# A gated cross-attention layer: the first loads in another order, two chunks of each half of x normalised by GpSimd, tables with gaps

## The reference

```
xn   = layernorm(x)
q    = rope(einsum(xn @ Wq.T, w_kc_q))           # 16 heads, 192 wide
kv   = rope(ctx)                                 # 64 wide
attn = softmax((q @ W_qr) @ (kv @ W_kr).T)
x    = x + tanh(g_xattn) * ((attn @ kv) @ w_kc_kv.T) @ Wo.T
p    = softmax(layernorm(x) @ router.T + bias)   # 64 experts, top 8
x    = x + tanh(g_ffn) * (layernorm(x) * sum(top8) + top8 @ expert_bias)
```

## Time and profile before

| | us |
|---|---|
| median of 3 timed runs | 270.83 (270.72 to 271.25) |
| the profiled execution | 271.7 |
| its span, first to last instruction | 269.9 |
| TensorE busy | 257.0 (95%), 1825 matmuls |
| VectorE busy | 187.4 (69%) |
| ScalarE busy | 152.9 (57%) |
| GpSimd busy | 139.5 (52%) |
| DMA moved | 12.50 MB |

### The profile page before, as it was taken

The page is one execution under the profiler, slowest core; times in us unless marked ns, Lnnn a source line. Parts: engine busy times, 40 slices in busy tenths (PEclk is TensorE's granted clock), DMA queues, the critical chain, the costliest instruction groups (busy, mean ns, idle before and its releaser), DMA issues.

```text
span 269.9 us, 5396 instructions
## 1 busy us (share of the span) xinstructions
PE 257.0 (95%) x1825; PEld 195.6 (72%) x1825; DVE 187.4 (69%) x434; ACT 152.9 (57%) x440; POOL 139.5 (52%) x223
## 2 busy tenths in 40 slices
PE   7899799999999999999999999999999999999963
PEld 7674678578867888587848888577848756888751
DVE  3689978485864877287829956488728956777675
ACT  2531574686545646375555575636646558878541
POOL 3197038623690468326652755337451883447353
PEclk9999799999999999999999999999999999999999
DMA  7995030415000000051000300000000000000103
GB/s 234 223 295 159 1 97 2 138 45 142 2 0 0 2 0 4 1 183 42 0 2 0 100 1 2 0 0 2 0 4 0 2 2 0 2 0 2 39 2 117
DMA packets 15434, 12.50 MB, mean 46 GB/s; under 512 B 4592, under 2 KB 14704, under 8 KB 15408
## 3 DMA queue, kind: packets, MB, share of 16 engines
q1 hardware_dynamic: 14304, 11.37, 15.2%
q10 hardware_dynamic: 1104, 0.79, 1.0%
HBM read 11.11 MB, written 1.05 MB: 45 GB/s over the span
## 4 chain that ended last, share of the span: by engine, by line
PE 74%; DVE 7%; POOL 6%; DMA 4%; issue 3%; ACT 3%; ACTq 1%; POOLq 0%; DVEq 0%
PE ring L1033 22%; PE context L1209 10%; PE probs_t L1191 9%; PE scores L1180 6%; PE scores L1181 5%; PE ring L1073 4%; PE ring L1059 4%; DMA rope_k_sb<-in_rope_k 4%; PE ring L999 3%; DVE q_stack L772 3%; PE ring L1094 2%; PE ring L1090 2%; PE ring L1092 2%; PE ring L1012 2%; PE ring L1022 2%
## 5 line engine op out<-in xcount | busy, mean ns | idle before, releaser
L596 POOL TENSOR_SCALAR probs<-probs,inv_sum 128x256 f32<-128x256 f32 x128 | 59.6, 480 | 82.7 <-DVE inv_sum L943 82.7
L540 POOL TENSOR_TENSOR roped<-roped,cross 128x512 f32<-128x512 f32 x47 | 59.9, 1296 | 22.9 <-DVE cross L786 22.7
L700 ACT ACTIVATE probs<-scores,neg_max 128x256 f32<-128x256 f32 x128 | 59.8, 476 | 14.9 <-DVE neg_max L937 14.6
L710 ACT COPY probs_t_sb<-probs_t 128x512 f32<-128x512 f32 x64 | 37.8, 590 | 39.8 <-PE probs_t L1191 39.2
L937 DVE TENSOR_REDUCE neg_max<-scores 128x2 f32<-128x512 f32 x64 | 43.3, 677 | 8.8 <-PE scores L1181 8.7
L1033 PE MATMUL ring<-xn_hi,a_hi 128*128 128x512 f32 x96 | 40.2, 418 | 0.0
L1191 PE MATMUL probs_t<-ident,probs 128*128 128x128 f32 x256 | 38.8, 274 | 0.2
L1180 PE MATMUL scores<-keys_hi,q_stack 128*128 128x256 f32 x128 | 38.1, 319 | 0.7 <-ACT probs L700 0.3
L772 DVE TENSOR_TENSOR q_stack<-ring,q_stack 64x512 fp32r<-64x512 f32 x32 | 22.0, 689 | 23.5 <-ACT q_stack L691 22.9
L785 DVE TENSOR_TENSOR roped<-ring,rope_q_sb 128x512 f32<-128x512 f32 x48 | 32.8, 684 | 7.1 <-PE ring L1033 6.6
L1033 PE MATMUL ring<-xn_hi,a_lo 128*128 128x512 f32 x96 | 37.7, 393 | 0.0
(11 more groups left out here) (105 smaller groups left out, 438.0 us busy)
## 6 DMA issues: line engine op xcount, KB each, us to landing
...
```

The source lines that it names most:

```text
L540: last = nc.gpsimd.tensor_tensor(roped[:, j, k, :], roped[:, j, k, :], cross[:, done % 2, j, :], ALU.add)
L596: last = nc.gpsimd.tensor_scalar(e, e, inv_sum[:, i % 4, half:half + 1], 1.0, ALU.mult, ALU.mult)
L700: last = nc.scalar.activation(probs[:, i % E_BUFS, half, :], scores[:, i % 2, half, :], ACT.Exp, bias=neg_max[:, i % 4, half:half + 1], ac ...
L710: nc.scalar.copy(probs_t_sb[:, i % T_BUFS], probs_t[:]).then_inc(probs_t_ready, 1)
```

## The change

SP now issues pair 1's key weights behind the query weights, then the context, the key tables, and only then the three query tables; ScalarE issues x (chunks 2, 3) and pair 0's key weights. The rows of rope_q_sb and w_qr_sb get a gap of 8 elements, so that a query table arrives in rows of 2 KB and not of 4 KB, and the rank weights in rows of 1.5 KB and not of 3 KB; the tables' layout in SBUF is indexed anew. In each half of x VectorE normalises chunks 0 and 1 (of four) and GpSimd adds eps, takes the power and normalises chunks 2 and 3, with a semaphore of its own, xn_by_pool. The order of pieces is new in the opening (among others, both key pieces behind the rank merge), in the slots and at the end. No matmul is added or taken away. Of the slots' lists the first two steps and the last are shown.

```diff
--- before.py
+++ after.py
@@ -34,6 +34,7 @@
 E_BUFS, T_BUFS = 4, 8
 BLOCK_OF = (0, 2, 1)
 SHARED_SUM = PC - 1
+PAD = 8
 LOWEST = float(np.finfo(np.float32).min)
 WARM_UP = 24
 LEAD = 2
@@ -59,9 +60,9 @@
 
 def pieces_before():
 
-    return [("n", 0), ("a", 0, 0), ("x", 0, 0), ("a", 0, 2), ("x", 0, 1), ("c",), ("a", 0, 3), ("a", 0, 1),
-            ("table", 0), ("half", 2), ("q", 0, 0, 0), ("q", 0, 0, 1), ("q", 0, 1, 0), ("table", 1), ("q", 0, 1, 1),
-            ("k", 1), ("table", 2), ("q", 0, 2, 0), ("q", 0, 2, 1), ("m", 0, 0), ("k", 0), ("n", 1), ("r", 0),
+    return [("n", 0), ("a", 0, 0), ("a", 0, 1), ("a", 0, 2), ("x", 0, 0), ("c",), ("a", 0, 3), ("x", 0, 1),
+            ("half", 2), ("table", 0), ("q", 0, 0, 0), ("table", 1), ("q", 0, 0, 1), ("table", 2), ("q", 0, 1, 0),
+            ("q", 0, 1, 1), ("q", 0, 2, 0), ("q", 0, 2, 1), ("m", 0, 0), ("k", 0), ("k", 1), ("n", 1), ("r", 0),
             ("p", 0), ("x", 1, 0), ("x", 1, 1), ("a", 1, 1)]
 
 
@@ -74,66 +75,66 @@
     (
         ([("a", 1, 0)], []),
         ([("q", 1, 0, 1)], [("q", 1, 1, 0)]),
-        ([("q", 1, 1, 1)], [("q", 1, 2, 0)]),
+        ([], [("q", 1, 1, 1), ("q", 1, 2, 0)]),
         ([("q", 1, 2, 1)], [("a", 1, 2), ("a", 1, 3)]),
         ([], [("r", 1), ("p", 1)]),
-        ([("o", 1, 0)], [("m", 1, 0)]),
-        ([], [("out", 0, 0, 2)]),
-        ([], [("q", 2, 0, 0)]),
+        ([("o", 1, 0)], []),
+        ([("m", 1, 0)], []),
+        ([("out", 0, 0, 2)], []),
     ),
     (
+        ([("q", 2, 0, 0)], []),
         ([], []),
-        ([], []),
-        ([("q", 2, 0, 1)], [("q", 2, 1, 0)]),
+        ([("q", 2, 0, 1), ("q", 2, 1, 0)], []),
         ([("q", 2, 1, 1)], [("q", 2, 2, 0)]),
-        ([("q", 2, 2, 1)], []),
+        ([], [("q", 2, 2, 1)]),
         ([("r", 2), ("p", 2)], [("out", 0, 2, 2)]),
-        ([("out", 1, 4, 2)], []),
-        ([("q", 3, 0, 0)], [("q", 3, 0, 1)]),
+        ([("out", 1, 4, 2)], [("q", 3, 0, 0)]),
+        ([("q", 3, 0, 1)], [("centre",), ("a", 2, 2)]),
     ),
...
     (
-        ([("turn", 0, 2)], []),
-        ([("root", 0, 2)], [("logit", 0, 2)]),
+        ([("root", 0, 2), ("turn", 0, 2)], []),
+        ([], [("logit", 0, 2)]),
         ([("out", 6, 2, 2)], []),
-        ([], [("take", 0, 2)]),
-        ([("turn", 2, 2)], [("pick", 0, 2), ("part", 0, 2), ("root", 2, 2)]),
-        ([], []),
-        ([("logit", 2, 2), ("out", 7, 4, 2)], []),
-        ([("turn", 4, 2), ("root", 4, 2)], [("take", 2, 2), ("mix", 0, 2), ("logit", 4, 2), ("take", 4, 2)]),
+        ([], [("turn", 2, 2), ("take", 0, 2)]),
+        ([("root", 2, 2)], [("pick", 0, 2)]),
+        ([("logit", 2, 2), ("part", 0, 2)], []),
+        ([("out", 7, 4, 2)], []),
+        ([("turn", 4, 2)], [("root", 4, 2), ("take", 2, 2), ("mix", 0, 2), ("logit", 4, 2), ("take", 4, 2)]),
     ),
 )
 
@@ -161,10 +162,10 @@
 
 def pieces_after():
 
-    return [("part", 2, 2), ("pick", 2, 2), ("pre", 7, 6, 2), ("out", 7, 6, 1), ("root", 6, 1), ("out", 7, 7, 1),
-            ("root", 7, 1), ("turn", 6, 1), ("part", 4, 2), ("logit", 6, 1), ("mix", 2, 2), ("take", 6, 1),
-            ("pick", 4, 2), ("part", 6, 1), ("turn", 7, 1), ("logit", 7, 1), ("take", 7, 1), ("pick", 6, 1),
-            ("mix", 4, 2), ("part", 7, 1), ("mix", 6, 1), ("pick", 7, 1), ("mix", 7, 1)]
+    return [("pick", 2, 2), ("part", 2, 2), ("pre", 7, 6, 2), ("out", 7, 6, 1), ("root", 6, 1), ("out", 7, 7, 1),
+            ("part", 4, 2), ("pick", 4, 2), ("root", 7, 1), ("turn", 6, 1), ("logit", 6, 1), ("take", 6, 1),
+            ("mix", 2, 2), ("turn", 7, 1), ("part", 6, 1), ("logit", 7, 1), ("pick", 6, 1), ("take", 7, 1),
+            ("mix", 4, 2), ("mix", 6, 1), ("pick", 7, 1), ("part", 7, 1), ("mix", 7, 1)]
 
 
 def ring_plan():
@@ -224,13 +225,13 @@
         x_sb = sb("x_sb", [P, CHUNKS, D])
         ctx_sb = sb("ctx_sb", [P, CHUNKS, DC])
         gates = sb("gates", [P, 2])
-        rope_q_sb = sb("rope_q_sb", [P, PC, 4, S])
+        rope_q_sb = sb("rope_q_sb", [P, PC, 2, 2 * S + PAD])
         rope_k_sb = sb("rope_k_sb", [P, 1, 2, 2, DC])
         wq_sb = sb("wq_sb", [P, GH, D])
         w_kc_q_sb = sb("w_kc_q_sb", [P, GH, CQ])
         w_kc_kv_sb = sb("w_kc_kv_sb", [P, GH, DC])
         wo_t_sb = sb("wo_t_sb", [P, GH, D])
-        w_qr_sb = sb("w_qr_sb", [P, 2, PC, P])
+        w_qr_sb = sb("w_qr_sb", [P, 2, PC * P + PAD])
         w_kr_sb = sb("w_kr_sb", [P, 2, P])
         w_kr_half = sb("w_kr_half", [P, 2, DC])
         router_t_sb = sb("router_t_sb", [P, 2, E])
@@ -313,6 +314,7 @@
         var_ready = sem("var_ready")
         rstd_ready = sem("rstd_ready")
         xn_ready = sem("xn_ready")
+        xn_by_pool = sem("xn_by_pool")
         key_products = sem("key_products")
         keys_ready = sem("keys_ready")
 
@@ -414,7 +416,7 @@
         def ranks_of(j, k, e):
 
             at = HALF * 2 * e + 64 * BLOCK_OF[k]
-            return w_qr_sb[:, j].rearrange("p k c -> p (k c)")[:, at:at + 64]
+            return w_qr_sb[:, j, at:at + 64]
 
         def load_x(queue, i):
             x_dram = x.rearrange("(c p) d -> p c d", p=P)
@@ -436,7 +438,7 @@
                             ).then_inc(wq_in[g], 16)
 
         def load_rank_weights(queue, g):
-            queue.dma_start(w_qr_sb[:], w_qr[g]).then_inc(wr_in[g], 16)
+            queue.dma_start(w_qr_sb[:, :, 0:PC * P], w_qr[g].rearrange("p j k c -> p j (k c)")).then_inc(wr_in[g], 16)
             queue.dma_start(w_kr_half[0:64], w_kr[g, 0:64, 0:2, 0:DC]).then_inc(wr_in[g], 16)
             queue.dma_start(w_kr_half[64:128], w_kr[g, 64:128, 1:3, DC:2 * DC]).then_inc(wr_in[g], 16)
             queue.dma_start(w_kr_sb[:], w_kr[g, :, 0:3:2, :]).then_inc(wr_in[g], 16)
@@ -444,7 +446,8 @@
         def load_rope(queue, k):
 
             table = rope_q[0:64, k] if k < 2 else rope_q[64:128, 0]
-            queue.dma_start(rope_q_sb[0:64, k], table).then_inc(rope_q_in[k], 16)
+            queue.dma_start(rope_q_sb[0:64, k, :, 0:2 * S], table.rearrange("p (i t) s -> p i (t s)", i=2)
+                            ).then_inc(rope_q_in[k], 16)
 
         def load_rope_keys(queue):
 
@@ -465,11 +468,12 @@
             load_x(sp, 0)
             for pair in range(2):
                 load_first_query_weights(sp, pair)
-            load_rope(sp, 0)
+            load_first_key_weights(sp, 1)
             sp.dma_start(ctx_sb[:].rearrange("p (b c) d -> p b c d", c=2),
                          ctx.rearrange("(b p c) d -> p b c d", p=P, c=2)).then_inc(ctx_in, 16)
-            load_rope(sp, 1)
-            load_rope(sp, 2)
+            load_rope_keys(sp)
+            for k in range(PC):
+                load_rope(sp, k)
             load_x(sp, 2)
             load_x(sp, 3)
             load_rank_weights(sp, 0)
@@ -532,6 +536,15 @@
                 pool.wait_ge(key_products, 2)
                 nc.gpsimd.tensor_copy(keys[:, :, 1, :], keys[:, :, 0, :]).then_inc(keys_ready, 1)
 
+            def normalise_tokens(t):
+
+                c = 4 * t + 2
+                pool.wait_ge(rstd_ready, c + 2)
+                for e in range(c, c + 2):
+                    last = nc.gpsimd.tensor_scalar(xn[:, e, :], x_sb[:, e, :], moments[:, e, 0:1], rstd[:, e:e + 1],
+                                                   ALU.subtract, ALU.mult)
+                last.then_inc(xn_by_pool, 2)
+
             def rope_sums(n, k, u):
 
                 done = n * PC + k
@@ -547,9 +560,13 @@
                         rope_context()
                     if piece[0] == "n":
                         for i in range(2 * piece[1], 2 * piece[1] + 2):
+                            pool.wait_ge(moments_ready, 2 * i + 2)
+                            nc.gpsimd.tensor_scalar(var_eps[:, 2 * i:2 * i + 2], moments[:, 2 * i:2 * i + 2, 1], EPS,
+                                                    1.0, ALU.add, ALU.mult).then_inc(var_ready, 2)
                             pool.wait_ge(var_ready, 2 * i + 2)
                             nc.gpsimd.tensor_tensor(rstd[:, 2 * i:2 * i + 2], var_eps[:, 2 * i:2 * i + 2],
                                                     minus_half[:, 0:2], ALU.pow).then_inc(rstd_ready, 2)
+                        normalise_tokens(piece[1])
                     if piece[0] == "q" and piece[3] == 1:
                         rope_sums(piece[1], piece[2], u)
                     if piece[0] == "part":
@@ -612,9 +629,7 @@
         @block.scalar
         def _(act):
             load_x(act, 1)
-            for pair in range(2):
-                load_first_key_weights(act, pair)
-            load_rope_keys(act)
+            load_first_key_weights(act, 0)
 
             def pieces(slot):
                 for u, piece in slot:
@@ -622,7 +637,8 @@
                     if kind == "table":
                         k = piece[1]
                         act.wait_ge(rope_q_in[k], 16)
-                        nc.scalar.copy(rope_q_sb[64:128, k], rope_q_sb[0:64, k]).then_inc(rope_q_ready, 1)
```

(17 more changed lines are left out.)

52 lines of the change are left out of this document (26 added, 26 removed).

## The result

| | before | after |
|---|---|---|
| median, us | 270.76 (20 runs, 269.50 to 273.06) | 272.77 (20 runs, 271.14 to 273.59) |
| profiled execution, us | 271.7 | 271.14 |
| its span, us | 269.9 | 269.3 |

The changed kernel is slower: ratio 1.0064 with a 95% interval of 1.0045 to 1.0083. The forecast was 269.5, faster, with a range that ended at 270.9. Note the profiled executions: by them alone the change would look like a gain of 0.6 us, while the medians show a loss of 2.0. The one shown of before is longer than 15 of the 20 timed beside the result, the one of after is the shortest of its 20. The ratios leave out the slow executions, those more than 1.5% above the fastest of the same kernel (6 of before's 33, one of e9's 12); the medians do not.

What follows compares the result with a forecast made beforehand. The loop was taken as bound by TensorE's matmuls. Opening -2.1, loop 0 and end +0.8 made -1.3 on a span of 269.9: 268.6, plus 0.9 for 269.5 us; range 268.0 to 270.9 (8 in 10).

Steps and rivals of the forecast that it cites:

- Normalising: Opening: GpSimd normalises two chunks per half at 0.55 us each; with the loads, products start at 10.5, gain 1.2 us.
- Rival (c): Opening: GpSimd's first-half chunks or the key tables come about 1 us late; 270.5 us, no change; chance 0.14.
- VectorE's first maximum: End of the opening: starts at 30.9 instead of 32.91 us; opening gain 2.0 to 2.2, 2.1 taken.
- The clock: Late opening: TensorE's fall to 1.2 GHz from about 29.96 to 33.4 us was taken to stay.
- Rival (a): Opening: the clock doesn't fall, so the opening is worth 3.0 us instead of 2.1; 268.6 us; chance 0.2.
- From span to median: Whole kernel: the median is the profiled span plus 0.9 us, so span 268.6 gives 269.5.
- Loads: Opening: pair 1's key weights land at 6.8 to 7.5 us, so its merge starts at 7.8 without waiting.
- Rival (d): Opening: pair 1's key weights, behind 768 KB on SP's queue, land no sooner; 271.5 to 272 us; chance 0.1.
- Keys moved: Opening: key products behind the rank merge remove waits of 0.38 and 0.30 us; rank products at 21.4, gain 1.9.
- Loop: Loop: value 0; bounds 1.0 us of idle to win and one exposed sum, 0.3 to 1.3, to lose.
- End: End: two swaps in VectorE's order cost 0.45 us each, less 0.1 of step 7; loss 0.8 (0 to 1.1).
- Rival (b): End: the new order costs nothing because another wait takes the addition's place; 268.7 us; chance 0.08.

Runs made afterwards that it cites:

- e9: The changed kernel with 30 unread identity transposes in TensorE's gap ahead of the second half of x; 271.17 us, ratio 1.0007.
- e2: The changed kernel with VectorE normalising all four chunks of each half again, GpSimd keeping eps and the power; 269.32 us, ratio 0.9917.
- e3: The changed kernel with GpSimd normalising by (add, mult) with a negated mean instead of (subtract, mult); 269.01 us, ratio 0.9933.
- e1: The changed kernel itself, run again as yardstick and for a second profile; 272.54 us, ratio 1.0039.
- e5: The kernel before with only the new order and queues of the first loads; 269.12 us, ratio 0.9911.
- e10: e3 with the first loads in the order and on the queues of the kernel before; 270.66 us, ratio 0.9992.
- e7: e3 with the end's order of pieces from the kernel before; 267.84 us, ratio 0.9873.
- e4: The changed kernel with the end's order of pieces from the kernel before; 271.52 us, ratio 1.0007.
- e11: e3 without the gaps, so query tables arrive in rows of 4 KB again; 269.02 us, ratio 0.9948.

## Why the prediction was wrong, and where it was right

**Normalising, the failed step.** The prediction put "its two chunks at 7.45 to 8.55 (2 x 0.55, the same kind with two scalars for each partition)". They started at 7.46 and took 2.44. The row was the same in engine, shape and type but not in the operations, and I did not count that as a difference. VectorE's own chunks are (subtract, mult), but no row of before shows GpSimd doing this on 128x256; the price was unknown and needed a bound above. Rival (c) had "GpSimd is late" with 1 us in the chain, from starts and tables that come late, and never from the instruction itself; its 270.5 is 2.3 us short. The Trainium skill, "GPSIMD Engine Reference", section "Engine selection", calls operations with one input on GpSimd roughly line-rate against VectorE. The runs show 1222 against 411 ns for (subtract, mult), a factor of 3.0, so the rule would have misled here too. GpSimd's 555 ns for (add, mult) come nearer to it, 1.35 times VectorE's 411; how long VectorE takes for (add, mult), no run shows.

**What it cost.** In the first half 0.99 us (e2 against after, with equal starts of the merges). In the second half TensorE waited until 29.78 where 27.3 was forecast. The next merge is 2.06 us later than in e3, and since the loop is bound by TensorE that goes into the time. The forecast followed VectorE's first maximum as the mark of the opening's end. That mark hides the loss: at the same clock (e1 against before) it is at 32.96 against 32.91, while TensorE's restart is 0.61 us later (30.45 against 29.84) and the merged output product 0.35.

**The clock, a term with the wrong size.** "I take the fall to stay" was true of after's executions but only of some of before's: its profile had the stretch at 1.2 GHz, while 15 of 33 executions, 4 of 11 beside e5 and 16 of 29 beside e10, have a mean clock of at least 0.996, which leaves no room for 3.4 us at half clock (1.7 of 270 us, a mean of 0.994). So about every second execution of before (35 of 73) was free of it, and after the change 4 of 20, and none of 12 in e1, by their spans. Only profiles show where a clock fell; for the others this is read from span and mean clock. Price 1.4 us. Rival (a), no fall, is what 7 of e3's 12 executions show, with the instruction time that the forecast assumed: its case was as likely as the forecast's, and e3's profile bears out its size, with the opening 3.1 us shorter (31.51 against 34.62) where (a) had 3.0. With the fall (e7's profile, 33.10) it is 1.5 shorter, not 2.1. In the changed kernel itself the idle stretch was longer than either had it. A second fall, under the last products of the end, is in no line of the forecast: it is in 3 of the 8 profiles with the new order at the end (e9's left aside), and costs 0.4 us (table below).

**From span to median, a second failed step.** "The median shown is 270.83, so the span plus 0.9." The time is nearly always the span plus 1.8, and the median of before is a span of 269.0. The 0.9 mixed that constant with the fact that the profiled execution was 0.9 us longer than the middle one. So the sum of -1.3 started from an execution with the fall and was carried over to a median in which about half have none.

**Loads: right.** The merge of pair 1 follows at once, as forecast; the key weights' landing was forecast at 6.8 to 7.5 and is 2.2 + 4.9 = 7.1. In one profile (e4) the merge still waited 0.60 us and started at 8.10. The context rotation starts at 9.86, straight behind the two chunks (forecast 10.1), and at 9.12 in e3, where the key tables release it. The gain is 1.66 us in e5's trace, where the forecast's terms for it are 1.2 and the 0.38 of the keys; with the new lists it is 1.28 in the traces (e10 against e3 at the merged output product) and 1.65 in the medians. Rival (d) did not occur. The reason that I gave for the old landing was in part wrong. The rule of turns packet by packet (the Trainium skill, "DMA: Bandwidth & Descriptors", section "Queues, rings and completion order") would explain it, I wrote, only if the table's 4 KB pieces had the larger turns. e10 has the late landing without such pieces, and e11 the early one with them. Why a third load on ScalarE's queue takes 7.5 us stays open; no run changed the queue alone.

**Keys moved: right.** From the first product to the rank products it took 22.33 - 11.88 = 10.45 us, forecast 10.9, before 11.55. The loads had half of that: in e5, with the old lists, the wait for the keys is gone too and it takes 21.60 - 10.59 = 11.01. The first product itself came 1.4 us later than forecast. About 0.4 of it is how late TensorE's warm-up ended in this execution (6.88, and 6.48 in the earlier trace rows; e3 had 6.23); the rest is mostly GpSimd.

**Loop: inside its bounds, but not 0.** TensorE is busy for 200.35 of 201 us, and one wait of 0.2 us for a sum is left, as in before. From the merged output product to the last attention product it takes 223.2 to 223.3 us with the new lists and 223.9 to 224.0 with the old: 0.7 us gained, where the forecast had 0.

**End: right in its mechanism.** Forecast loss 0.8, by two swaps of 0.45; measured 0.78 in the traces (e1 against e4), 1.0 in the medians, and 1.2 between e3 and e7, the fall at the end included. From the last attention product to the end it is 12.2 us (257.1 to 269.3) in the profile of after, forecast 11.9, but 0.4 of it is that fall; without it (e1) it is 11.8. Rival (b) did not occur.

**The account.** Stages of the profiled executions in us, cut at the start of the first merged output product and at the start of the last attention product on TensorE:

| | opening | loop | end | span | fall to 1.2 GHz under products |
|---|---|---|---|---|---|
| before | 34.62 | 224.00 | 11.3 | 269.9 | opening |
| e5, new loads only | 31.97 | 223.93 | 11.3 | 267.2 | nowhere |
| e1, changed kernel | 34.97 | 223.28 | 12.05 | 270.3 | opening |
| after, changed kernel | 33.56 | 223.26 | 12.5 | 269.3 | end |
| e2, VectorE normalises | 32.21 | 223.30 | 12.1 | 267.6 | nowhere |
| e3, (add, mult) | 31.51 | 223.19 | 12.5 | 267.2 | end |
| e10, e3 with old loads | 32.79 | 223.27 | 12.5 | 268.6 | end |
| e4, old end | 34.79 | 223.33 | 11.3 | 269.4 | opening |
| e7, (add, mult) and old end | 33.10 | 223.16 | 11.2 | 267.5 | opening |

At the same clock (before and e1) the changed kernel loses 0.35 in the opening and 0.8 at the end and wins 0.7 in the loop, 0.4 us in all. The medians are 2.0 us apart (1.4 in e1's group). What the falls explain of the difference is an estimate: the opening's in 28 of 32 executions of the changed kernel and at most 38 of 73 of before, at 1.4 us, makes 0.5, and the end's at most 0.4. The remaining 0.7 us or more (0.1 in e1's group) stays open. The 7 longest of after's 20 executions (spans of 271.3 to 271.8) have a mean clock of 0.986 or 0.987, which no profile of the changed kernel shows. The lists were not run alone; their 0.7 in the loop is read from traces, of which only two have the old lists.
